# Causal attention's second pass: masks by a minimum on VectorE instead of matmuls, and the orders of the engines' work written anew

## What is computed

```python
q, k, v = heads(Wq, x), heads(Wk, x), heads(Wv, x)     # 16 heads of 8
score = jnp.einsum('bhnd,bhmd->bhnm', q, k) * scale
causal = jnp.tril(jnp.ones((S, S), dtype=bool))
score = jnp.where(causal, score, -jnp.inf)
attn = jax.nn.softmax(score, axis=-1)
out = jnp.einsum('bhnm,bhmd->bhnd', attn, v)
```

## Time and profile before

| | us |
|---|---|
| median of 3 runs (2063.61 to 2066.46) | 2063.85 |
| the profiled execution | 2061.38 |
| its span, first to last instruction | 2059.3 |
| TensorE matmuls busy | 1616.5 (78%) |
| VectorE busy | 1121.5 (54%) |
| ScalarE busy | 1015.8 (49%) |
| GpSimd busy | 605.5 (29%) |
| mean granted TensorE clock | 0.91 |

### The profile page before, as it was taken

The page is one execution under the profiler, slowest core; times in us unless marked ns, Lnnn a source line. Parts: engine busy times, 40 slices in busy tenths (PEclk is TensorE's granted clock), DMA queues, the critical chain, the costliest instruction groups (busy, mean ns, idle before and its releaser), DMA issues.

```text
span 2059.3 us, 32978 instructions
## 1 busy us (share of the span) xinstructions
PE 1616.5 (78%) x11554; PEld 941.5 (46%) x11632; DVE 1121.5 (54%) x2562; ACT 1015.8 (49%) x2297; POOL 605.5 (29%) x400
## 2 busy tenths in 40 slices
PE   1666688986889768895889868897699957898579
PEld 1334244553546435562445535463355625455235
DVE  3443492746646474644927466464837449274514
ACT  1435246653657327472466536573374724665041
POOL 5624060513315051420605033150515106051000
PEclk9787789997999889997999979999899979999689
DMA  4010200112002120113101120021201130011301
GB/s 127 19 23 1 59 23 2 50 51 62 21 1 65 50 47 21 28 46 77 31 2 49 51 62 21 1 65 51 47 21 34 49 79 20 2 49 44 62 2 51
DMA packets 37330, 80.69 MB, mean 39 GB/s; under 512 B 6766, under 2 KB 22638, under 8 KB 33760
## 3 DMA queue, kind: packets, MB, share of 16 engines
q1 hardware_dynamic: 37136, 78.22, 14.8%
HBM read 54.74 MB, written 8.78 MB: 31 GB/s over the span
## 4 chain that ended last, share of the span: by engine, by line
PE 43%; DVE 17%; ACT 14%; issue 13%; POOL 10%; DMA 1%; SPq 1%; DVEq 0%; POOLq 0%; ACTq 0%
PE ps L324 37%; PE ps L329 6%; ACT work L718 4%; DVE cmax L1032 4%; POOL work L1178 4%; ACT big L785 4%; POOL small L1155 3%; DVE small L934 2%; POOL work L1189 2%; DVE work L903 2%; ACT L807 1%; ACT L718 1%; ACT big L807 1%; DVE work L902 1%; DVE small L910 1%
## 5 line engine op out<-in xcount | busy, mean ns | idle before, releaser
L324 PE MATMUL ps<-bxt,mw 128*128 128x512 f32 x576 | 276.6, 604 | 3.7 <-ACT big L807 3.7
L324 PE MATMUL ps<-maskb,identb 128*128 128x128 bf16 (+1 forms) x1106 | 228.7, 239 | 27.9 <-ACT work L718 16.4
L718 ACT ACTIVATE work<-ps,pbias,small 128x128 f32<-128x128 f32 x512 | 226.1, 473 | 48.0 <-DVE pbias L938 47.5
L1155 POOL TENSOR_TENSOR brs<-bmv,consts 128x4 f32<-128x4 f32 x16 | 3.2, 202 | 754.3 <-DVE bmv L843 754.3
L324 PE MATMUL ps<-wqkv,h 128*128 128x512 f32 x384 | 199.4, 651 | 30.9 <-ACT v L680 11.0
L1032 DVE TENSOR_REDUCE cmax<-ps 128x1 f32<-128x384 f32 (+3 forms) x352 | 204.3, 630 | 29.7 <-PE ps L324 29.6
L1178 POOL TENSOR_TENSOR work<-work 128x1024 f32<-128x1024 f32 x64 | 150.7, 2354 | 232.2 <-DVE work L903 231.6
L1155 POOL TENSOR_TENSOR small<-small,consts 128x8 f32<-128x8 f32 x128 | 208.2, 1640 | 2.6 <-DVE small L912 2.6
L324 PE MATMUL ps<-pk,pq 96*128 96x512 bf16 (+3 forms) x512 | 139.6, 329 | 79.6 <-DVE cmax L1032 54.7
L329 PE MATMUL ps<-ident,work 128*128 128x128 f32 x1056 | 169.4, 307 | 40.0 <-DVE work L979 12.9
L785 ACT ACTIVATE big<-ps 128x512 f32<-128x512 f32 x320 | 163.9, 634 | 57.0 <-PE ps L324 56.9
(11 more groups left out here) (162 smaller groups left out, 2611.0 us busy)
## 6 DMA issues: line engine op xcount, KB each, us to landing
mw<-in_experts SPq DMA_DIRECT2D x72, 384.0 KB, 3.0
pk<-scr_parts SPq DMA_DIRECT2D x48, 192.0 KB
pq<-scr_parts SPq DMA_DIRECT2D x144, 64.0 KB
v<-v SPq DMA_DIRECT2D x16, 512.0 KB, 4.5
v<-v SPq DMA_DIRECT2D x16, 384.0 KB, 5.8
scr_parts<-big SPq DMA_DIRECT2D x8, 768.0 KB, 3.9
xin<-in_x SPq DMA_DIRECT2D x8, 256.0 KB, 4.4
out<-x SPq DMA_DIRECT2D x8, 256.0 KB, 3.1
```

The costliest lines, as they stand in the source:

```text
L324: return nc.tensor.matmul(o, a, b, start=start, stop=stop, skip_group_check=True)
L718: i = nc.scalar.activation(pr[:, m, a, p, :], fb[2 * (m % 2) + a][:, p * P:(p + 1) * P], ACT.Exp, bias=pbias[:, m, k:k + 1], scale=rn[:, m ...
L1155: return nc.gpsimd.tensor_tensor(out, x, consts[:, k:k + 1].broadcast_to([x.shape[0], x.shape[1]]), op)
```

## The change

TensorE no longer adds the mask in pass 2. The exponentials of the future are then whatever comes, infinity included. VectorE takes, behind each exponential and in place, the lesser of the diagonal blocks and a bound: 2^100 for the past and the diagonal, 0 for the future. `EXP_DIAGONALS` gives a fill's one or two diagonal blocks: 128 columns in 4 fills of a group, 256 in 6. A new semaphore `c_cut` counts 40 of these in a sequence, and the first product of a group waits for ten of it as well as for its ten exponentials. VectorE's back half has 40 more units, so its order has 214 letters instead of 174; the orders of TensorE (240), ScalarE (150) and SyncE (15) have the same units in another sequence, GpSimd's is the same.

```diff
+BOUND = 2.0 ** 100
...
+EXP_DIAGONALS = [slice(0, 1) if len(f) == 1 else slice(0, 4, 3) if f[0][1] == 1 else slice(0, 3, 2) for f in EXP_FILLS]
...
-        causal_qk, causal_kq = maskb[:, 2 * T:2 * T + P], maskb[:, 2 * T + P:2 * T + 2 * P]
+        causal_qk, bound_kq = maskb[:, 2 * T:2 * T + P], maskb[:, 2 * T + P:2 * T + 2 * P]
...
+        c_cut = sig("c_future_cut", 4 * 10)
...
-                            mm(bank[:, at:at + cols], pk[r][:, hh, kk * P:(kk + 1) * P], pq[r][:, hh, kk * P:T], stop=False)
-                            i = mm(bank[:, at:at + P], identb[:, :], causal_kq, start=False)
+                            i = mm(bank[:, at:at + cols], pk[r][:, hh, kk * P:(kk + 1) * P], pq[r][:, hh, kk * P:T])
...
                                 pe.wait_ge(c_e.sem, c_e.at(s, 10 * (gg + 1)))
+                                pe.wait_ge(c_cut.sem, c_cut.at(s, 10 * (gg + 1)))
...
-                yield "maxturn.1"
-                split_maxima(1, bb[3])
+                for k in range(4 * len(EXP_FILLS)):
+                    if k == 3:
+                        yield "maxturn.1"
+                        split_maxima(1, bb[3])
+                    n = k % len(EXP_FILLS)
+                    yield f"s{k // 10 % 2}{n}.{k // 20}"
+                    blocks = big[:, n, :].rearrange("p (a b) -> p a b", b=P)[:, EXP_DIAGONALS[n], :]
+                    dve.wait_ge(c_e.sem, c_e.at(s, k + 1))
+                    tt_(blocks, blocks, bound_kq.unsqueeze(1).broadcast_to(blocks.shape), ALU.min).then_inc(c_cut.sem, 1)
...
-    kept = np.concatenate([first] * 4 + [keep] * 4 + [k <= q, q <= k], 1)
-    return np.where(kept, 0.0, NEG).astype(np.float32)
+    kept = np.concatenate([first] * 4 + [keep] * 4 + [k <= q], 1)
+    return np.concatenate([np.where(kept, 0.0, NEG), np.where(q <= k, BOUND, 0.0)], 1).astype(np.float32)
```

More of the change, by code:

```diff
@@ L49 @@
 ORDER = {
[L50 to L56, removed]
+    "tensor": "BBFFFFFFFFFBFFFBFBFFBBBFFFBFBBFFBBFFBBBBBBFBBBFBBBBFBBBFBBBBFBFBBFBBFBBBFBBBFFBBBFBBBBBFBBBBBBFBBBBB"
+        "BBFBBBBBBBBBBBBBBBBBBBBBBBBBBBFBBBBBFFFBFFBBFBBBBBBBBBBFFBFBBBBFBFBBBBBBBFBBBFFFBFFFBFBBFFBBBBBBBFBB"
+        "BFBFBBBBBFFFFFFBFFBBFBFBFBBBFBBBFFFFFFFF",
+    "scalar": "BBFFFFFFFFFFFFFFFFFFFFFFFFFFFFFFFFFFFFFFFBBBBBBBBBBFBBBBBBBBBBBFBBBBBBBBBBBFBBBBBBBBFFFBBBBBFFFFBFBB"
+        "BFFFBBFBFFFBFFBFBFBFBBFFFFBBFFFFFFFBFFFFBBBFBFFFFF",
+    "vector": "BBFFBBBBFFFFBFFFFFFFFBFFFBFFBFFFFFFBBBBBFBFBBBBFBBFBBFBBBFBBFBFBBBBFBFFFBBBBBFBBBBBFBBBBBBBBBBBFBBBB"
+        "BBBFBBBBBBBBBBBBBBBFBBBBBFFBBBFBBBBBBBFBBBBBBFBFFBBFBBBBBFFBBFFBBFFFFFFBBBFBFFBBBFFBFBFBFBFFFFFBFBBB"
+        "FFBBBBBFBFFFFF",
     "gpsimd": "BFFFFFFFFFFFFFFFFFFFBFFFFFFFFFFFFFFFFF",
-    "sync": "FBBFBBBFBBBBBBB",
+    "sync": "FBFBBBBBBFBBBBB",
 }
```

## The result

| | before | after |
|---|---|---|
| median of the runs, us | 2064.95 | 2108.86 |
| ratio to before, with its 95% interval | 1 | 1.0211 [1.0194, 1.0229] |
| span of the profiled execution, us | 2059.3 | 2105.5 |
| a turn of the loop (mean of seven), us | 239.64 | 245.09 |
| the last back half, from its first copy to the end, us | 154.4 | 161.4 |

The change costs 2.1%, 44 us, where a gain of 9 was forecast, and the time lies above the range. The first row to read is again the copy at the head of the back half. Its eight starts divide the 46.2 us by which the span grew: seven turns of (1944.1 - 228.5) / 7 = 245.09 us instead of 239.64, 38.1 us; the last back half 7.0; the first front half 1.1.

A forecast was written before the change was run, and what follows sets the result against it. Stages of a turn have different limits; pass 2 runs on ScalarE's exponentials, TensorE's product and handovers. Per turn -2.2 - 0.5 + 1.0 = -1.7, seven turns -12, last back half +3: -9 us, 2055 from 2063.85; range 2030 to 2078.

The forecast's parts named there:

- the walk of the new orders: Step-by-step timing of a turn's new sequence through pass 2 to layer 1's first projection: lead of 2.2 us a turn.
- the clock term: Allowance for TensorE's clock falling in pass 2 once it has less work: +1.0 us a turn.
- Part 1: Pass 2's 64 mask matmuls a turn leave TensorE: 3.5 us of its time, worth 0 to 3.5 us a turn.
- Part 2: VectorE's bound in pass 2: only each group's last is exposed, 0.5 us four times, +2.0 us a turn (1.2 to 3.3).
- lag behind the exponentials: Sign of being wrong, in pass 2: VectorE's bounds falling behind ScalarE's exponentials instead of keeping step with them.
- Part 3: New orders on every engine but GpSimd: -2.2 us a turn, parts 1 and 2 included, and -0.5 for table loads.
- the list of what would prove it wrong: Signs: a turn under 236 or over 240 us, lagging bounds, pass 2 starting after 552, or clock at 1.00 throughout.
- the table loads: ScalarE's order in layer 1 needs one table change fewer each way: -0.5 us a turn (ends 0 and -2.6).
- Part 4: TensorE's clock in pass 2 may drop towards 1.2 GHz: +1.0 us a turn (0 to 9.4), +1 in the last half.
- The rival that named this: Clock falls at the ends of groups 2 and 3: 2092 us at worst, 2072 with one product per turn; chance 0.22.

The follow-up runs named there:

- e3: The kernel before, its orders kept, with pass 2's mask matmuls removed and no minimum put in: 2056.86 us, ratio to before 0.9965.
- e2: The changed kernel's new orders, but masks by matmul as before, without the minimum or its wait: 2090.26 us, ratio to before 1.0137.
- e4: The changed kernel's new orders, with neither mask matmuls nor minimum in pass 2: 2102.42 us, ratio to before 1.0189.
- e1: The kernel before, its orders kept, with VectorE's minimum in place of the mask matmuls: 2075.14 us, ratio to before 1.0051.
- e11: Masks by matmul; new orders up to the first expert, except layer 0's w1, w1a, w2 at old places; orders of before from there: 2076.99 us, ratio 1.0069.
- e9: The changed kernel plus six idle matmuls of 512 columns ahead of the waits of each group's product: 2102.88 us, ratio to before 1.0188.
- e13: The changed kernel plus 32 idle matmuls of 512 columns at the start of each turn: 2099.65 us, ratio to before 1.0168.
- e14: The kernel before plus 32 idle matmuls of 512 columns at the start of each turn: 2047.85 us, ratio to before 0.9934.
- e15: The changed kernel with the product's single wait for ten minima split into waits for 7, 9 and 10: 2064.28 us, ratio to before 1.0010.

## Why the prediction was wrong

The step that failed is the walk of the new orders: it gave a lead of 2.2 us a turn where the orders lose 3.9. The second is the size of the clock term.

**Part 1** (3.5 us of TensorE, worth 0 to 3.5 a turn). In the orders of before it is worth 1.0 a turn (e3 against before), of which 0.7 is two long starts fewer. In the new ones it is below the lower end: -1.55 a turn (e2 to e4). About half of that is the slow product, 1.5 us, less what the masks' absence saves in the other groups, between turns with a long start (245.0 to 245.7); the other half is that e4 has no short start. The bound was drawn from the masks' own time and left no room below nothing, because the effect on the clock stood in part 4 alone.

**Part 2** (2.0 us a turn exposed) was right in the rows of the last half: durations 0.29 and 0.42 as in the sum, the product 0.56 us behind the exponentials (2012.75 against 2007.18 + 5.01), the gap ahead of it 0.62 longer. The lag behind the exponentials, one of the signs of being wrong, is there in the loop and off the path. In the loop e1 over e3 is +2.07 a turn, and that this meets the 2.0 is luck: e1 has five long starts and e3 one, which makes some 1.5 of it, and between turns with a short start the minimum costs about 0.6. In the new orders it adds nothing to the turn (245.13 and 245.09): there the turn is set by something else.

**Part 3** (the lead of 2.2 us) is the step that failed. The walk had the sequence right and the times late, step by step, in us behind the turn's first copy:

| | before | predicted | after |
|---|---|---|---|
| group 1's exponentials | 81.1 | 82.2 | 85.5 |
| group 2 | 90.1 | 91.1 | 95.1 |
| group 3 | 99.9 | 100.5 | 105.0 |
| group 4 | 108.0 | 108.9 | 113.6 |
| output transposes | 117.5 | 122.4 | 128.0 |
| layer 1's first projection | 132.3 | 128.3 | 134.6 |

3.3 us are lost ahead of pass 2, and that was on the list of what would prove it wrong. Half is the turn's start: the first rotary product comes 29.6 us into the turn instead of 27.9, and the stretch at the low clock there lasts to 30.1 us instead of 27.7. The walk started from a turn of before with a short start, and all seven of after have a long one. The rest was the copies and units ahead of the last maximum: e2's turn in the same place has a short start (28.0) and still begins pass 2 at 83.7, its turns with a long start at 85.5 to 85.7. The groups, with the slow product in group 2, add 1.4 up to group 4, and what is behind it 0.9 (the stretch with the Gelus took 10.4 us against 10 predicted; the third Gelu's 0.69 us stands in the trace and not in rows 4). And the lead wasn't kept afterwards: the new tail cost 1.7 us a turn where 0.5 was to be gained. So the orders cost 3.9 a turn (e2), where the walk, with parts 1 and 2 in it, and the table loads gave -2.7.

**Part 4** (the clock: +1.0 a turn, +1 in the last half) was the right mechanism, undersized in the last half. The 0.94 of the last back half was taken as proof that such a stage holds its clock; but the masks were in it. Without them it was 0.79 with products of 3.8 to 4.05 us. With the bound the four groups take 7.8 us more, and pass 2 begins 0.9 earlier: the last half is +7.0 instead of +3. A product at the low clock was put at 4.7 us; the longest measured is 4.17 (e4), because the low stretch covers only a part of it. The rival that named this (2072 to 2092) had the last half at +7 and half a product to two products a turn, where e2 to e4 show 1.55; what it lacked is that this adds to orders that lose by themselves. What the Trainium skill says ("TensorE: Matmul & The Clock Gate", section "Part 1: The HAM clock gate"), that throttled is the default and activity releases the clock, agrees with these rows: 0.94 with the masks, 0.79 without.

**The sum** by what was measured, in medians: new orders +25, masks away +12, minimum +6, together the +44.

**The +2.1 of the pass 1 and pass 2 orders** (e11) is for the most part starts: four more long ones than before are worth some 1.4 a turn, and between long turns e11 takes 242.0 to 242.6 us where before takes 241.7.

**What stays open.** Why the new orders make a long start more frequent isn't shown. And after, e4, e9 and e13 settle at nearly the same turn, 245.6 to 246.0 us from the second to the sixth, whatever their start and wherever a product is slow. From the output transposes to the next copy it is 117.4 to 117.8 us in after, e4 and e13, so for these three the sameness arises ahead of the transposes. That a turn and the places where the clock falls hold each other fits (e13 is 2 us ahead at the first rotary product and has lost it by the end of pass 2, with two products at 4.05), but no run shows it.

## What to carry to other kernels

Before small matmuls are taken off TensorE in a stage that another engine bounds, read the granted clock of that stage and ask what keeps it up: here masks that were off the chain kept the last half's products, which are on it, at 2.36 us instead of up to 4.17. Split a wait for "all ten" by what the first consumer really reads; that was worth 0.5 to 2.0% here (9.5 to 41 us) and cost two lines. And price orders with the clock held (work left in, only the order changed), or the clock will hide one part's gain in another's loss. And where turns of a loop come in two kinds, compare like with like before a difference of means is given to an edit.

## What was unexpected of the hardware

Matmuls whose result nobody reads made the kernel faster: 32 of 512 columns a turn brought a stretch of eleven us from 0.53 to 1.00 granted clock and the time down by 0.7%, 14 us (e14). Six ahead of each product took 1.6 us off a group that is on the path. The clock fell in stretches in which TensorE was far from idle: it was busy for 14 of 18.5 us in the stretch of after with 0.91. Just ahead of the fall in it, from 572.9 to 576.3, it was busy for 1.58 of 3.40 us, with no idle time longer than the 1.72 us ahead of the product, and then the product ran at 0.50. And in one execution, with the same instructions in every turn, the turns come in two lengths, 1.9 to 2.7 us apart (before, e1, e2, e15), by how long the low clock at their start lasts.
